# First attention: pieces of the running maxima at other places among a step's scores, closing and turning transposes beside the values, softmax sums turned by four-column products

## The reference, cut to what matters

```
q = _qdq(x) @ _qdq(wq).T + bq
kv = cond @ wkv.T + bkv
k, v = jnp.split(kv, 2, axis=-1)
q = q.reshape(B, N, H, Dh)
k = k.reshape(B, M, H, Dh)
v = v.reshape(B, M, H, Dh)
scale = 1.0 / np.sqrt(Dh)
attn = jax.nn.softmax(jnp.einsum('bnhd,bmhd->bhnm', q, k) * scale, axis=-1)
o = jnp.einsum('bhnm,bmhd->bnhd', attn, v).reshape(B, N, C)
out = _qdq(o) @ _qdq(wp).T + bp
```

## Time and profile before

| What | Value |
|---|---|
| median of three runs | 2582.68 us |
| profiled execution, its own time | 2584.68 us |
| its span | 2582.9 us |
| TensorE busy | 2515.3 us (97%) |
| VectorE busy | 1788.7 us (69%) |
| ScalarE busy | 1233.5 us (48%) |
| GpSimd busy | 1287.2 us (50%) |
| granted TensorE clock, mean | 0.996 of full |
| one L1332 reduction | 980 / 988 / 995 ns (least, median, most), 480 of them |

### The profile page before, as it was taken

The page is one execution under the profiler, slowest core; times in us unless marked ns, Lnnn a source line. Parts: engine busy times, 40 slices in busy tenths (PEclk is TensorE's granted clock), DMA queues, the critical chain, the costliest instruction groups (busy, mean ns, idle before and its releaser), DMA issues. The chain is left out here.

```text
span 2582.9 us, 33907 instructions
## 1 busy us (share of the span) xinstructions
PE 2515.3 (97%) x13273; PEld 1624.9 (63%) x13288; DVE 1788.7 (69%) x2455; ACT 1233.5 (48%) x1853; POOL 1287.2 (50%) x340
## 2 busy tenths in 40 slices
PE   8999999999999999999998999999999999999998
PEld 8988888987544545545544787888533333334786
DVE  4554554556767767767774676674799999999873
ACT  3221312311666666666664232322588888886110
POOL 0000000000999999999994000000499999997310
PEclk9999999999999999999999999999999999999999
DMA  8677776655535345345313753542997777776400
GB/s 301 215 249 241 263 277 240 220 180 156 107 80 119 72 87 112 72 93 109 68 66 114 261 183 135 181 155 79 251 213 165 167 160 167 157 173 192 126 33 33
DMA packets 218864, 405.10 MB, mean 157 GB/s; under 512 B 18216, under 2 KB 94536, under 8 KB 218640
## 3 DMA queue, kind: packets, MB, share of 16 engines
q1 hardware_dynamic: 218704, 402.93, 56.4%
HBM read 260.63 MB, written 140.59 MB: 155 GB/s over the span
## 5 line engine op out<-in xcount | busy, mean ns | idle before, releaser
L1458 POOL TENSOR_TENSOR pooled<-pooled,probs 128x2048 f32<-128x2048 f32 x140 | 641.1, 4579 | 21.0 <-POOL pooled L1458 0.9
L1305 ACT ACTIVATE probs<-psum 128x512 f32<-128x512 f32 (+1 forms) x832 | 458.7, 598 | 338.8 <-PE psum L1196 334.2
L1332 DVE TENSOR_REDUCE win_max<-psum 128x1 f32<-128x802 f32 x480 | 455.4, 988 | 151.4 <-PE psum L1161 151.0
L2236 DVE TENSOR_SCALAR probs<-psum,bound 128x1024 f32<-128x1024 f32 (+1 forms) x416 | 498.9, 1274 | 31.3 <-POOL pooled L2268 19.5
L2211 ACT ACTIVATE probs<-probs 128x1024 f32<-128x1024 f32 (+1 forms) x416 | 437.6, 1059 | 82.2 <-DVE probs L2236 40.6
L2268 POOL TENSOR_TENSOR pooled<-pooled,probs 128x2048 f32<-128x2048 f32 x92 | 424.2, 4610 | 12.8 <-ACT probs L2211 0.2
L1196 PE MATMUL psum<-q_st,k_st 128*128 128x512 f32 (+1 forms) x832 | 334.6, 439 | 18.5 <-ACT probs L1305 12.1
L296 POOL TENSOR_TENSOR r_q<-ve_q,minus_half 128x4 f32<-128x4 f32 x8 | 9.1, 1132 | 611.3 <-DVE ve_q L256 611.3
L1196 PEld LDWEIGHTS psum<-q_st,k_st 128*128 128x128 f32 (+1 forms) x832 | 149.1, 185 | 240.8 <-ACT probs L1305 179.2
L1161 PE MATMUL psum<-k_st,q_st 96*128 96x402 f32 x960 | 266.7, 359 | 6.1 <-DVE o_sb L1363 5.1
L2179 PE MATMUL psum<-q_st,k_st 128*128 128x512 f32 (+1 forms) x832 | 250.7, 426 | 12.9 <-DVE probs L2236 9.8
(11 more groups left out here) (271 smaller groups left out, 4281.8 us busy)
## 6 DMA issues: line engine op xcount, KB each, us to landing
k_st<-k_hi SPq DMA_DIRECT2D x64, 801.0 KB, 9.2
k_st<-k_lo SPq DMA_DIRECT2D x48, 801.0 KB, 11.0
k_hi<-kt_hi SPq DMA_DIRECT2D x32, 801.0 KB, 3.6
k_lo<-kt_lo SPq DMA_DIRECT2D x32, 801.0 KB, 5.8
v_rows<-v_out SPq DMA_DIRECT2D x96, 256.0 KB
v_st<-v_rows SPq DMA_DIRECT2D x24, 768.0 KB
q_st<-q_hi SPq DMA_DIRECT2D x64, 256.0 KB, 7.9
w<-w_hi_d SPq DMA_DIRECT2D x64, 256.0 KB, 3.1
```

The source lines that it names most:

```text
L1305: A.activation(probs[i % NPROBS][0:rows, j, :], bank(score_banks.where["score", u, t, j])[0:rows, :], ACT.Exp, scale=1.0 / ROOT).then_inc( ...
L1332: V.tensor_reduce(win_max[:, r, j, c:c + 1], window(windows.where["max", u, i])[:, :, 0:MV], AX.XY, ALU.max).then_inc(max_done, 1)
L1458: G.tensor_tensor(pooled[u % 2][:], before[:], probs[tile(u, k) % NPROBS][:], ALU.add).then_inc(pool_added, 1)
L2236: V.tensor_scalar(probs[i % NPROBS][0:rows, half * W:half * W + W, :], window(("score", u, t, half))[0:rows], bound[0:rows, u // NG, t:t + 1],
```

## The change

On TensorE the second piece of a step moves from ahead of the values to behind S2, and the third from ahead of S3 to behind S3. Closing and turning move from behind S3 to right behind the values, ahead of S2. VectorE's order follows: one reduction ahead of the closing arithmetic and two behind it, where there were three ahead. The sums are no longer transposed: `den_sb` is multiplied with four columns of the identity (each 32nd), so that 16 columns come out next to each other, and the reciprocal reads those.

```diff
@@ closing, TensorE @@
-                        for w, src in enumerate((acc_sb, den_sb)):
-                            for r in range(RT):
-                                m = M.transpose(window(slot)[:, w, r * P:(r + 1) * P], src[:, r * P:(r + 1) * P],
-                                                ident[:])
+                        for r in range(RT):
+                            M.transpose(window(slot)[:, 0, r * P:(r + 1) * P], acc_sb[:, r * P:(r + 1) * P], ident[:])
+                        for r in range(RT):
+                            m = M.matmul(window(slot)[:, 1, r * HPG:(r + 1) * HPG], den_sb[:, r * P:(r + 1) * P],
+                                         ident[:, 0:P:DH], start=True, stop=True)
@@ a step, TensorE @@
                         if now:
                             scores(*now, 1)
-                        if coming[1:]:
-                            max_of(*coming[1])
                         if behind:
                             values(*behind)
                             if behind[1] == LAST_SUM and behind[0]:
                                 last_sum(behind[0] - 1)
                         if now:
-                            scores(*now, 2)
-                        if coming[2:]:
-                            max_of(*coming[2])
-                        if now:
-                            scores(*now, 3)
                             if now[1] == CLOSE_AT and now[0]:
                                 closing(now[0] - 1)
                             if now[1] == TURN_AT and now[0] + 1 < UNITS:
                                 turn(now[0] + 1)
+                            scores(*now, 2)
+                        if coming[1:]:
+                            max_of(*coming[1])
+                        if now:
+                            scores(*now, 3)
+                        if coming[2:]:
+                            max_of(*coming[2])
@@ closing, VectorE @@
-                        s = own.after(V.reciprocal(rec[:], ps[:, 1, 0:S:DH].rearrange("p (r j) -> p r j", j=HPG)))
+                        s = own.after(V.reciprocal(rec[:], ps[:, 1, 0:RT * HPG].rearrange("p (r j) -> p r j", j=HPG)))
@@ a step, VectorE @@
-                        if now and now[0] + 1 < UNITS:
-                            for i in windows_at(now[1]):
-                                max_of(now[0] + 1, i)
+                        coming = [(now[0] + 1, i) for i in windows_at(now[1])] if now and now[0] + 1 < UNITS else []
+                        for one in coming[:1]:
+                            max_of(*one)
                         if now and now[1] == CLOSE_AT and now[0]:
                             closing(now[0] - 1)
+                        for one in coming[1:]:
+                            max_of(*one)
```

## The result

The changed kernel takes 2621.66 us (median of four runs, 2618.92 to 2622.33) against 2583.45 us before: ratio 1.0145, 95% interval 1.0133 to 1.0158. It is slower by 38.2 us; forecast were 2624 us and 41.5 us more. The profiled execution took 2621.65 us with a span of 2619.8 us, so spans grew by 36.9 us.

The account below looks back on a forecast made before the run. TensorE's order was taken to set the 47.85 us unit, GpSimd a floor 0.75 below. Terms of 2.73 a unit, with the end units, gave 41.5 us more: 2626.2 profiled, a 2624 us median, range 2600 to 2642.

Parts of the forecast that it names:

- TensorE sets the unit, GpSimd is a floor near 47.1 us: Stage before: TensorE's order sets the 47.85 us unit; GpSimd, waiting 0.75 us, would take about 47.1.
- A window comes back after 1.62 us, and the score taken out of that time stands bare: Steps 5 to 10: first to third piece stays 1.62, an uncovered score adds 0.235; 3.75 a step, +1.19 a unit.
- The rival in which the window does not wait: Third piece finds its window free, step 3.33, GpSimd's floor limits the gain: some -15 us, 2568; chance 0.10.
- The sign named beforehand: Profile after: each step's third piece waits about 0.5 for VectorE in its load, in eight or nine steps instead of five.
- Two-bank and sums' steps: Steps with two score banks or carrying sums: 2 to 3 +0.16; three sums' steps 4.60 each, +0.45 together.
- Closing: Steps 4 to 5: the block behind the values delays VectorE's chain and the next window; 5.51 against 4.75, +0.76.
- The larger bound: Closing's eight small-product instructions: 0.11 each, 0.89 us in all, taken rather than nothing as the lower bound.
- Turning: Steps 11 to 12: turning now precedes all four scores, ahead of the wait for ScalarE; 3.11 against 2.57, +0.54.
- 12 to 0 and 10 to 11: Ends of the piece series: 12 to 0 loses the second piece, -0.37; 10 to 11 gains one inside ScalarE's wait, 0.
- The sum: 2.73 a unit, 38.2 over units 1 to 14; unit 0 1.9, unit 15 1.0, last closing 0.4; together 41.5 us.
- The rival of more waits: Closing leaves VectorE behind for several steps or turning misses its columns: another 1 to 1.5 a unit, 2643; chance 0.11.
- The rival of cheap products: Small products cost next to nothing (-0.89 a unit), half the turning loss hidden: 1.6 a unit remain, 2607; chance 0.18.

Follow-up runs that it names:

- the shorter reduction: Changed kernel with each of VectorE's 480 reductions over one bank of its window instead of both, leaving out half the context rows: 2573.15 us, ratio 0.9959.
- the wide places: Kernel before, with four scores and a piece between the piece behind the values and its window's next user, in steps 5 to 10: 2572.64 us, ratio 0.9958.
- The run with ten tiles: Against the wide places: GpSimd adds ten tiles of a unit instead of eleven, TensorE sums the eleventh with ones: 2573.07 us, ratio 0.9959.
- the exchange of one piece with one score: Changed kernel with the first piece behind the second score instead of ahead of it, in each step: 2595.33 us, ratio 1.0047.
- the run with turning alone: Kernel before with only turning moved, from behind the fourth score of step 11 to right behind the values: 2588.83 us, ratio 1.0022.
- the kernel with closing alone: Kernel before with only closing moved right behind the values in step 4, VectorE's closing one reduction earlier: 2582.85 us, ratio 1.0000.

## Why the prediction was right

The predicted time, 2624, is 2.3 us above the measured median, and the direction and the mechanism hold, step by step. The time is closer than the working deserves. The growth was forecast at 41.5. The traced spans grew by 36.9, which is 4.6 less; the medians are 38.2 apart, and the base that the forecast started from, 2582.68, lay 0.8 below the median of four runs. That both bring the forecast nearer is luck.

- **TensorE sets the unit, GpSimd is a floor near 47.1 us.** Shown: GpSimd's idle time grew from 0.75 to 3.29 us a unit, and in the two kernels that freed TensorE (the shorter reduction, the wide places) the first full units lasted 46.0 to 46.2; once TensorE had met GpSimd most lasted 47.0 to 47.1, and the load of `last_sum` waited for GpSimd. The run with ten tiles does not count for this: its 47.02 are TensorE's own.
- **A window comes back after 1.62 us, and the score taken out of that time stands bare.** Shown three ways: the return stayed at 1.62 in the profile after, the exchange of one piece with one score brought 3.52 back, and a shorter reduction brought 3.33. The rival in which the window does not wait had its step at 3.33; it came true only where the reduction was halved. The sign named beforehand was a wait in eight or nine steps of a unit, about 0.5 long; it is in ten (148 over 15), 0.64 long in a full step.
- **Two-bank and sums' steps take the same form.** Right to 0.03 us a step.
- **Closing.** Forecast 5.51, measured 5.37. The step mis-sized is the block: 1.00 + 0.10 + 0.44 + 0.89 = 2.43 behind the values; it was 2.30 (946.95 to 949.25), 0.49 for the four transposes with their exposed load and 0.81 for the eight small ones. The larger bound was the right choice for them. Both terms were too large because 0.27 was taken off for the last instruction of a row; starts alone, which were there to read, give 0.36 for four (887.35 to 887.71) and 0.81 for the eight of the earlier trace rows (107.07 to the next product at 107.88). The Trainium skill, TensorE: Matmul & The Clock Gate, section LDWEIGHTS (loading the stationary operand), gives 107 ns for a load of 128 columns; the rows give 0.10 an instruction, which fits. The Trainium skill, TensorEngine Tiling (Array Packing), section Instruction Overhead, gives a product about 60 cycles; the eight would be 0.2 us by that, an estimate from its figure, and they took 0.81, so here the measurement decides.
- **Turning.** Forecast 3.11, measured 2.95: the first score came 1.40 behind the values, not 1.54, the same over-count of four transposes. The mechanism is shown by the run with turning alone. The 0.65 for freeing a bank was read up to a load (912.10) that shows no wait, which gives an upper bound only; it held, since the load that does wait after the change gives 0.65 too (975.63 to 976.28).
- **12 to 0 and 10 to 11.** Right to 0.01.
- **The sum.** A unit grew by 2.46 between step 2 of unit 1 and step 2 of unit 15 (34.4 us over 14), not 2.73; unit 0 by 2.2 and unit 15 by 1.0, against 1.9 and 1.0. The values of step 2 of unit 0 came 0.7 earlier than before (639.27 against 639.95). That is probably not the change. TensorE waits at the start of the stage, first 2.78 and then 1.32 us, and its granted clock is then 0.50, the 1.2 GHz level; between 637 and 639 us it is 0.83 before and 1.00 after. In the kernel with closing alone, whose first two steps are as before, it is 1.00 from 635 on and the values come at 639.14. So the 0.7 is within what unchanged steps vary by. The last closing cost 0.35 (forecast 0.4). 34.4 + 2.2 + 1.0 + 0.35 - 0.7 gives 37.3 for a span that grew by 36.9.
- **The rival of more waits** had one true part: closing behind the values delays two pieces in a row, which costs nothing with the pieces at their old places and 0.1 to 0.2 a unit with them moved, not 1 to 1.5. The forecast had counted it. The rival of cheap products was wrong.

## What to carry to other kernels

When two buffers rotate between a producer and a consumer, measure the return time of a buffer, then count what the producer has to do between its use and its reuse. Work inside that time, up to its length, is free, and in a step that this wait binds, work taken out of it is paid in full. Here one matmul of 0.235 us on the wrong side cost 0.24 us in five steps of each unit, and four scores inside that time instead of three made the kernel faster until the next engine's floor. A transpose block put in front of work that another engine waits for is paid even if it used to be hidden behind it. Fewer output columns do not make a product cheaper when it needs as many weight loads: at 4 and at 128 columns an instruction took 0.10 us here. And measure a run of short instructions from start to start, not by the length of its row.

## What the runs showed of the hardware that I had not expected

A four-column fp32 product costs slightly more array time than two 128-column transposes of fp32. The four products are eight instructions and took 0.81 us, 0.20 each; the four transposes are four instructions and took 0.36, 0.09 each. Only the end is quicker: VectorE's reciprocal, at 949.50, started 0.25 behind the block's end, where it had started 0.35 behind that of the transposes (887.71 to 888.06).

A weight load that is shown to wait need not cost that much. At 968.50 above the load had waited 1.71 us and the array 0.80, because the products ahead of it were still running.
